# Two convolutions of an attention branch in two halves of the TensorE array

## What is computed

```python
def cab(x, p):                      # x: (B, 128, 64, 64)
    t = gelu(conv2d(x, p['cab_w1'], p['cab_b1'], 1))      # 3x3, 128 -> 42 channels, exact Gelu
    t = conv2d(t, p['cab_w2'], p['cab_b2'], 1)            # 3x3, 42 -> 128 channels
    s = t.mean((2, 3), keepdims=True)
    s = relu(conv2d(s, p['ca_w1'], p['ca_b1'], 0))        # 1x1, 128 -> 4
    s = sigmoid(conv2d(s, p['ca_w2'], p['ca_b2'], 0))     # 1x1, 4 -> 128
    return t * s
# in the block: x = x * skip_scale2 + cab(layernorm(x))
```

## Time and profile before

| | us |
|---|---|
| median of 3 runs | 16634.83 (16606.00 to 16645.12) |
| the profiled execution | 16628.47 |
| its span | 16626.2 |
| TensorE busy | 12916.6 |
| VectorE busy | 11319.8 |
| ScalarE busy | 9624.6 |
| GpSimd busy | 5738.2 |
| mean granted TensorE clock | 0.784 of full speed |

### The profile page before, as it was taken

One profiled execution on the slowest core, in us unless ns is written; L12 is line 12 of the kernel. 1 busy time (PEld: TensorE's weight loads), 2 busy tenths in 40 slices (PEclk: granted clock), 3 DMA queues, 4 the chain that ended last, 5 costly groups with the idle time before them and its releaser, 6 DMA issues.

```text
span 16626.2 us, 190937 instructions
## 1 busy us (share of the span) xinstructions
PE 12916.6 (78%) x48256; PEld 7971.4 (48%) x48256; DVE 11319.8 (68%) x15030; ACT 9624.6 (58%) x20979; POOL 5738.2 (35%) x4760
## 2 busy tenths in 40 slices
PE   5778878787787877878788787877878778787735
PEld 4454554545445354554545545454453545545312
DVE  3584875848668485784848758486684857848585
ACT  1375664747657375674756647475574756747433
POOL 6451441514325052341514425153250523415100
PEclk7868778787786978778687787877869688786857
DMA  5442332423234142332423324232341423324100
GB/s 163 117 126 72 108 103 77 125 76 105 86 98 123 57 126 71 111 112 68 125 73 108 101 82 126 70 108 83 98 123 58 125 72 111 112 68 124 55 1 13
DMA packets 662188, 1561.60 MB, mean 94 GB/s; under 512 B 76952, under 2 KB 347484, under 8 KB 650556
## 3 DMA queue, kind: packets, MB, share of 16 engines
q0 software_dynamic: 368640, 1208.25, 25.2%
q1 hardware_dynamic: 289980, 302.80, 6.1%
q10 hardware_dynamic: 2304, 33.56, 0.5%
HBM read 1338.15 MB, written 206.14 MB: 93 GB/s over the span
## 4 chain that ended last, share of the span: by engine, by line
PE 37%; DVE 29%; DVEq 13%; issue 10%; ACT 6%; POOL 2%; DMA 1%; ACTq 1%; SPq 0%; POOLq 0%
PE psum L1291 6%; PE psum L1168 6%; DVEq L933 6%; PE psum L1102 4%; DVE arena L937 4%; PE psum L1300 4%; DVE arena L900 3%; DVE arena L942 3%; DVE arena L894 3%; DVE arena L896 3%; DVE arena L959 3%; DVEq L925 2%; DVE arena L905 2%; PE psum L1112 2%; DVE arena L922 2%
## 5 line engine op out<-in xcount | busy, mean ns | idle before, releaser
L657 POOL DMA_INDIRECT gathered<-cell_table,index_now x2880 | 3206.1, 1113 | 3079.3 <-PE psum L1102 2100.4
L657 POOL DMA_INDIRECT arena<-cell_table,index_now x1440 | 2039.0, 1416 | 2279.7 <-PE psum L1102 1980.2
L440 ACT COPY samples_t<-psum 128x384 f32<-128x384 f32 x1536 | 717.5, 467 | 2589.0 <-PE psum L1102 2348.4
L1201 PE MATMUL psum<-arena,pack 32*128 32x512 f32 x1024 | 912.0, 986 | 1610.0 <-DVEq L956 1568.3
L1112 PE MATMUL psum<-samples_t,pack 128*128 128x128 f32 x9216 | 1867.4, 387 | 273.7 <-ACT samples_t L440 273.7
L1102 PE MATMUL psum<-pack,gathered 128*128 128x128 f32 x11520 | 1602.6, 300 | 488.4 <-DVE gathered L836 402.9
L1112 PEld LDWEIGHTS psum<-samples_t,pack 128*128 128x128 f32 x9216 | 1742.5, 292 | 464.5 <-ACT samples_t L440 464.5
L1102 PEld LDWEIGHTS psum<-pack,arena 128*128 128x128 f32 x6912 | 1330.4, 217 | 1025.4 <-issue 1025.2
L1102 PE MATMUL psum<-pack,arena 128*128 128x128 f32 x6912 | 1544.5, 410 | 326.5 <-DVE arena L1028 235.4
L1102 PEld LDWEIGHTS psum<-pack,gathered 128*128 128x128 f32 x11520 | 1486.1, 158 | 617.9 <-issue 614.7
L453 ACT ACTIVATE arena<-arena,weight_now 128x128 f32<-128x128 f32 x5760 | 1734.3, 390 | 7.7 <-DMA arena<-cell_table,index_now 7.6
(11 more groups left out here) (165 smaller groups left out, 21500.9 us busy)
## 6 DMA issues: line engine op xcount, KB each, us to landing
cell_table<-arena SPq DMA_DIRECT2D x64, 2112.5 KB
gathered<-cell_table,index_now POOLq DMA_INDIRECT x2880
arena<-in_x SPq DMA_DIRECT2D x16, 2048.0 KB, 7.6
image<-in_x SPq DMA_DIRECT2D x16, 2048.0 KB, 7.6
x_dram<-image SPq DMA_DIRECT2D x16, 2048.0 KB, 10.2
arena<-x_dram SPq DMA_DIRECT2D x16, 2048.0 KB, 7.9
out<-arena ACTq DMA_DIRECT2D x16, 2048.0 KB, 7.2
arena<-cell_table,index_now POOLq DMA_INDIRECT x1728, 3.7
```

Of the source, the lines that this page charges most:

```text
L657: pool.indirect_dma_start(gathered[m][:, n * CORNERS * C:(n + 1) * CORNERS * C], None, table, bass.IndirectOffsetOnAxis(ap=index_now[:, pa ...
L1201: pe.matmul(psum[:, B_BANK, :], row_of(high, n), part_of(proj_b[high, :], k, c), start=True, stop=True).then_inc(S["b_done"], 1)
```

## The change

Both convolutions take two pieces at a time (`p` counts 4 pairs, `i` the two pieces of a pair).

- First convolution: the weights are 128 rows by 42 columns, without the copy. Piece i of the pair writes PSUM partitions i * 64 to i * 64 + 41, in a bank of its own, so that it uses columns i * 64 and on of the array. The two pieces alternate tap by tap. Four banks are used: `hidden_bank(q)` is 0, 1, 4, 5 and again. A pair waits for three normalised pieces (the first), five and so on, and from the third pair on for the Gelus of the pair before the last.
- Gelu: ScalarE reads each piece's 42 partitions twice and writes the same values, unshifted, into `hidden_v[0:42]` and `hidden_v[64:106]`.
- Second convolution: 9 taps on 42 rows instead of 6 products on 106. Piece i of the pair takes its data and weights from partitions i * 64 to i * 64 + 41, so from rows i * 64 and on of the array, and writes bank 2 + i. A pair waits until both pieces of the pair before have been evacuated.
- `hidden_done` and `branch_done` rise by 2 behind each pair, on the last matmul of the second piece. The order and number of ScalarE's operations stay.
- The weights are laid out anew: `cab1` is smaller, `cab2` has 9 taps, twice (rows 0 to 41 and 64 to 105).

```diff
-        cab2 = carve(SCR + L, CM2, PAIRS * C)
-        cab1 = carve(SCR + L + PAIRS * C, 128, TAPS * CM2)
+        cab2 = carve(SCR + L, CM2, TAPS * C)
+        cab1 = carve(SCR + L + TAPS * C, 128, TAPS * CM)
...
+        def hidden_bank(q):
+
+            return q // 2 % 2 * 4 + q % 2
...
-                    act.activation(inner_rows(hidden_v[0:CM, :, :], q), wide(psum[0:CM, q % 2, :]), ACT.Gelu, bias=cab1b[0:CM, 0:1])
-                    act.activation(hidden_v[HALF:CM2, 1 + 8 * q:9 + 8 * q, 0:W], wide(psum[HALF:CM2, q % 2, :]), ACT.Gelu,
-                                   bias=cab1b[HALF:CM2, 0:1]).then_inc(S["hidden_ready"], 1)
+                    half = slice(q % 2 * HALF, q % 2 * HALF + CM)
+                    src = wide(psum[half, hidden_bank(q), :])
+                    act.activation(inner_rows(hidden_v[0:CM, :, :], q), src, ACT.Gelu, bias=cab1b[half, 0:1])
+                    act.activation(inner_rows(hidden_v[HALF:CM2, :, :], q), src, ACT.Gelu, bias=cab1b[half, 0:1]).then_inc(S["hidden_ready"], 1)
...
-                for q in range(CH):
-                    pe.wait_ge(S["ln_ready"], (2 * b + 1) * CH + min(q + 2, CH))
-                    if q >= 2:
-                        pe.wait_ge(S["hidden_ready"], b * CH + q - 1)
+                for p in range(CH // 2):
+                    pe.wait_ge(S["ln_ready"], (2 * b + 1) * CH + min(2 * p + 3, CH))
+                    if p >= 2:
+                        pe.wait_ge(S["hidden_ready"], b * CH + 2 * p - 2)
                     for n in range(TAPS):
-                        last = pe.matmul(psum[0:CM2, q % 2, :], cab1[:, n * CM2:(n + 1) * CM2], tap_rows(padded_v, q, n),
-                                         start=n == 0, stop=n == TAPS - 1)
-                    last.then_inc(S["hidden_done"], 1)
-                for q in range(CH):
-                    pe.wait_ge(S["hidden_ready"], b * CH + min(q + 2, CH))
-                    if q >= 2:
-                        pe.wait_ge(S["branch_ready"], b * CH + q - 1)
-                    for n in range(PAIRS):
-
-                        last = pe.matmul(psum[:, 2 + q % 2, :], cab2[:, n * C:(n + 1) * C], tap_rows(hidden_v, q, n // 2 * 3 + n % 2 * 2),
-                                         start=n == 0, stop=n == PAIRS - 1)
-                    last.then_inc(S["branch_done"], 1)
+                        for i in range(2):
+                            q = 2 * p + i
+                            last = pe.matmul(psum[i * HALF:i * HALF + CM, hidden_bank(q), :], cab1[:, n * CM:(n + 1) * CM],
+                                             tap_rows(padded_v, q, n), start=n == 0, stop=n == TAPS - 1)
+                    last.then_inc(S["hidden_done"], 2)
+                for p in range(CH // 2):
+                    pe.wait_ge(S["hidden_ready"], b * CH + min(2 * p + 3, CH))
+                    if p >= 1:
+                        pe.wait_ge(S["branch_ready"], b * CH + 2 * p)
+                    for n in range(TAPS):
+                        for i in range(2):
+                            q, half = 2 * p + i, slice(i * HALF, i * HALF + CM)
+                            last = pe.matmul(psum[:, 2 + i, :], cab2[half, n * C:(n + 1) * C], tap_rows(hidden_v[half, :, :], q, n),
+                                             start=n == 0, stop=n == TAPS - 1)
+                    last.then_inc(S["branch_done"], 2)
```

More of the change, by code:

```diff
@@ L54 @@
 CM2 = HALF + CM
-PAIRS = 6
 OB = 32
@@ L1368, in layout @@
         dtw[:, k, :, k] = a["L1_conv_dt_w"][k].reshape(2, C, R).transpose(0, 2, 1)
[L1369 to L1375, removed]
+    cab1 = a["L1_conv_cab_w1"].reshape(CM, C, TAPS).transpose(1, 2, 0)
+    cab2 = np.zeros((CM2, TAPS, C), np.float32)
+    cab2[:CM] = cab2[HALF:] = a["L1_conv_cab_w2"].reshape(C, CM, TAPS).transpose(1, 2, 0)
     cab1b = np.zeros((CM2, 1), np.float32)
```

## The result

The changed kernel takes 16,379.3 us (median of four runs; 16,359.0 to 16,407.3) against 16,635.4, which is the median of four runs too: the ratio is 0.985, with an interval of 0.9837 to 0.9862. It is faster, but by 256 us and not by the 531 that were forecast; it lies between the two forms of rival B and outside the range. The profiled execution took 16,384.0 us, 244.5 less than the one of before.

A forecast was written before the change was run, and what follows sets the result against it. TensorE's unbroken work in both convolutions was taken to set each image's end. Savings of 30.6 + 3.4 - 0.8 = 33.2 us an image, 531 us over 16, took 16628.5 to 16097, stated as 16,100 us; range 16,045 to 16,240.

The forecast's parts named there:

- rival B: Second convolution: the clock falls at the new gaps; 72 us (16,170) if it recovers, 371 us (16,470) if not; chance 0.11.
- First convolution, column halves side by side: First convolution: two column halves overlap fully, 72 slots of 0.429 us instead of 144 passes; 30.6 us saved an image.
- Rivals A and C: First convolution: A, weight loads in the way, 127 us (16,225), chance 0.13; C, column halves don't overlap, 16,590, chance 0.05.
- The estimate from the figure for column tiles: First convolution: 2.38 times for three column tiles would make a slot 0.54 us in place of 0.429, supporting rival A.
- Second convolution, row halves side by side: Second convolution: row halves overlap fully; 30.9 + 1.2 late starts + 5.7 gaps = 37.8 us against 41.2, 3.4 saved an image.
- The end: Behind the second convolution's last pair: ScalarE evacuates two pieces instead of one, 0.8 us lost an image.
- The clock: Both convolutions: passes priced at granted clock 1.00, 0.429 us each, with second-convolution gaps of 1.91 us costing only their length.
- its large form: Second convolution: the clock doesn't come back before the end, three pairs at twice the time; 371 us, 16,470.
- Nothing outside moves by more than some 10 us: Outside the two convolution stages: a larger move than this would mean the forecast is wrong as a whole.
- Rival D: Both convolutions: matmuls with 42 columns or rows don't lift the clock; 429 us slower, 17,060; chance 0.09.
- The order rule: Both convolutions: the second half starts one pass behind the first, 0.13 us at each of five starts; 10 us, 16,110.

The follow-up runs named there:

- the run with taps in blocks: Changed kernel with four output banks, second convolution doing all 9 taps of a pair's first piece before the second's; 17,039.1 us, ratio 1.0239 to the kernel before.

## Why the prediction was wrong

- **First convolution, column halves side by side: right.** 32.71 us against 32.4 forecast; 30.6 us saved an image, as the sum said. Rivals A and C fall: the slot stays at 0.43, with two loads in each, as these loads of one stretch show. The estimate from the figure for column tiles (the Trainium skill, "TensorE: Matmul & The Clock Gate", "Measured speedup vs the span model"), 0.54 us a slot, is not what happens here.

```profile
15400.28 0.12 PEld L1297 LDWEIGHTS psum<-padded,arena 128*42 128x42 f32 x2 [0.31 <-issue]
15400.72 0.12 PEld L1297 LDWEIGHTS psum<-padded,arena 128*42 128x42 f32 x2 [0.31 <-issue]
```

- **Second convolution, row halves side by side: right.** 18 slots of a pair take 7.95 us less the drain at its end, and from start to start a pair has 9.63 us with its gap. Forecast were 7.7 + 0.3 + 1.9 = 9.9; the late start of the second half isn't there (the two halves' first passes start within 0.01 us), and two pieces take ScalarE 1.46 us and not 1.56. In full, 36.8 us were to be had against 37.8 in the sum.
- **The end: right.** ScalarE's two pieces take 1.46 us against 0.78 for one: 0.7 us more, 0.8 forecast.
- **The clock: this is the step that failed.** The sum priced the new gap at 1.91 us and every pass at the upper level. The mechanism stood there as rival B, with its rows, but with a chance of 0.11, and its large form at 0.04 and outside the range. What happened is the large form, a clock that doesn't come back before the end, but not always from the first gap on. What the time came to: 58% of 1152 slots (16 images of 72) at 0.427 us more are 285 us; added up piece by piece it is 282. The terms with their measured sizes give 30.6 + 4.4 - 0.7 = 34.3 us an image, 549 in all; less 282, and less the 24 us of the next point, 243. The profiled executions differ by 244.5.
- **"Nothing outside moves by more than some 10 us": by this sign too the forecast was wrong.** Summed over the 16 images of the two profiled executions, the first convolution is 489.5 us shorter, the second 210.4 longer, and all the rest 34.7 longer. 11 of these are the longer end, forecast as 13; 24 are left. In an earlier stage the matmuls on 96 rows ran a little more often at the lower level. Rows of before, and of the changed kernel:

```profile
L1072 PE MATMUL psum<-padded,pack 128*96 128x512 f32 x768 | 364.6, 613 | 0.0
L1082 PE MATMUL psum<-pack,arena 96*128 96x27 f32 x1024 | 156.1, 318 | 0.0
```

```profile
L1076 PE MATMUL psum<-padded,pack 128*96 128x512 f32 x768 | 373.7, 626 | 0.0
L1086 PE MATMUL psum<-pack,arena 96*128 96x27 f32 x1024 | 169.1, 333 | 0.0
```

  That is 22 us more, and it is 22 too in the run with four banks (376.6 and 166.6), which came out 27 us above its expectation; the run with 64 rows has 361.5 and 149.3, 10 us less than before, and hit its expectation. The code of that stage is the same in all. But these matmuls are not the whole of it: in the run with the short gaps in the kernel before they take only 4 us more (369.0 and 156.1), and yet all that lies outside the convolutions is 30 us longer than before (that execution was 29 us above the median of its kernel). Executions of one and the same kernel differ too, by 39 us before and 48 us after. How much of the 24 us is due to the change, and how much to the execution that was profiled, stays open. That the stages only begin at other moments relative to the clock's changes is my reading; no run tests it.
- **Rival D** fell for both convolutions, but its mechanism is real: a single half of 42 rows does lose the clock, as the run with taps in blocks shows.
- **The order rule** (the Trainium skill, "TensorE: Matmul & The Clock Gate", "The mechanism": matmuls start and end in program order) is not borne out across row groups. In the changed kernel the second half doesn't start one pass behind the first, which was priced at 0.13 us: the loads of the second convolution begin with four, for two passes of each half, and go on by twos.

```profile
15427.42 0.30 PEld L1307 LDWEIGHTS psum<-arena 42*128 42x128 f32 x4 [0.83 <-issue]
15427.96 0.19 PEld L1307 LDWEIGHTS psum<-arena 42*128 42x128 f32 x2 [0.24 <-issue]
```

  And in the run with taps in blocks passes of the second piece begin beside the last passes of the first, before the last three of these have begun. The lead is only some four passes.

Why I misjudged B: I compared the gap of 1.9 us with a stretch that kept its clock with more idle time, 4.05 us in 10, and that stretch had matmuls on 128 rows. The stretch in the last rows of the same group, much of it with 32-row matmuls, lost it with less idle time, 2.2 us in 6.5. The changed kernel has both features, and I weighed them one by one. And I priced a fall by the start of the first convolution (1.5 us), where full-height matmuls brought the clock back; whether the new matmuls could do that was a question of its own.

## What to carry to other kernels

Halves of the array, by columns or by rows, run float32 matmuls fully side by side if they alternate in the program, and even nine products on 42 rows then beat six on 106. But when rows are given up, look at what the clock does: keep the stream free of gaps (more PSUM banks, here worth 363 us, of which about 90 is the length of the gaps themselves), or fill the rows up with zeros, which cost nothing that could be measured and brought 300 us. The best version here, four banks, takes 16,017 us, 3.7% under the kernel before; with 64 rows as well it is 16,007, which can't be told from it.

## What the runs showed of the hardware

- Matmuls with 42 columns in each half began at granted clock 0.50 in 15 of 16 images and had 1.00 again within the first convolution; those with 42 rows in each half never rose from 0.50 in up to 15.7 us of unbroken work. In the run with taps in blocks, where mostly one half of 42 rows works at a time, it stayed at 0.50 for 88 us. Few columns and few rows are not the same to the clock.
- Added rows that hold only zeros change what the clock does: 42, 53 and 64 rows in each half, with the same gaps, gave 16,379, 16,094 and 16,079 us.
- Gaps of 0.96 us in 106-row matmuls left the clock alone in all 16 images; gaps of 1.63 us, in the form with the two pieces in turn, lost it in every image, at 29 of 48 gaps, and each loss cost 1.7 us.
- Passes on two groups of rows overlap only near each other in the program: 18 passes of one half in front of 18 of the other overlapped by some four at each boundary.
